# Splitting the schedule's items of a fused attention and mixing layer, and new orders for all five engines

## The reference

```
x + attention(xn) + channel_mix(xn)

attention: q, k, v = silu(conv4(xn W))           causal depthwise convolutions of 4 taps
           beta = sigmoid(xn Wb); q, k of unit length
           delta rule over chunks of tokens: attn = inverse of (I + lower part of beta k k^T),
             u = attn v - (attn k) S, o = q S + (q k^T masked) u, S = S + k^T u
           ms = (conv3, conv15, conv31 of v, per channel) @ kernel_mix, then @ channel_mixer
           weights = softmax(gelu([xn, mean|ms|, mean|o|, mean|v|] W1 + b1) W2 + b2)   per head, 3 each
           out = rmsnorm(w0 ms + w1 o + w2 v) @ Wo
channel_mix: r = sigmoid(mix_r(xn) Wr), k = relu(mix_k(xn) Wk)^2, out = r * (k Wv)
             mix(x)_t = mu x_t + (1 - mu) x_(t-1)
```

## Time and profile before

| | us |
|---|---|
| three runs, median (lowest to highest) | 3507.43 (3506.42 to 3511.52) |
| the profiled execution, span from first to last instruction | 3507.7 |
| TensorE matmul busy, share | 3329.3, 95% |
| TensorE weight load busy | 2457.7, 70% |
| VectorE busy | 3165.0, 90% |
| ScalarE busy | 2760.5, 79% |
| GpSimd busy | 826.6, 24% |
| mean granted TensorE clock | 0.984 of full |

### The profile page before, as it was taken

How to read it: one execution, slowest core, us unless ns; L and a number is a source line. 1 busy time by engine, 2 the same in 40 slices (tenths; PEclk the granted TensorE clock), 3 DMA queues, 4 the chain that set the end, 5 groups by cost and what they waited for, 6 DMA issues and landing times.

```text
span 3507.7 us, 70018 instructions
## 1 busy us (share of the span) xinstructions
PE 3329.3 (95%) x22880; PEld 2457.7 (70%) x22880; DVE 3165.0 (90%) x7841; ACT 2760.5 (79%) x9146; POOL 826.6 (24%) x1501
## 2 busy tenths in 40 slices
PE   7999999999999999999999999999999999999988
PEld 6666777677776677776677766777766777766764
DVE  6998999999988999899999989999899999999994
ACT  5777888777887778887788877788877788777775
POOL 3322221122221222211222212222112222122211
PEclk9999999999999999999999999999999999999999
DMA  6012211122211222111222112222112221112211
GB/s 187 19 39 51 51 40 34 29 51 51 50 32 29 42 51 51 38 35 29 51 51 49 32 26 46 51 51 41 33 29 51 51 50 33 33 38 51 45 30 21
DMA packets 188307, 154.92 MB, mean 44 GB/s; under 512 B 111804, under 2 KB 146108, under 8 KB 187688
## 3 DMA queue, kind: packets, MB, share of 16 engines
q0 software_dynamic: 31744, 79.70, 13.2%
q1 hardware_dynamic: 156200, 70.76, 7.7%
HBM read 51.34 MB, written 52.95 MB: 30 GB/s over the span
## 4 chain that ended last, share of the span: by engine, by line
PE 35%; ACT 22%; DVE 21%; issue 9%; DMA 8%; POOL 4%; SPq 0%; ACTq 0%; DVEq 0%; POOLq 0%
DVE my L1804 16%; PE dense L798 7%; PE dense L732 5%; PE dense L736 5%; DMA my<-prod 5%; PE dense L720 3%; ACT my L1272 3%; PE small L748 2%; ACT dense L1302 2%; PE cell L702 2%; DMA rows_out<-Bm 2%; PE cell L703 2%; PE cell L695 2%; POOL Xu L464 1%; DMA Bu<-rows_out 1%
## 5 line engine op out<-in xcount | busy, mean ns | idle before, releaser
L1804 DVE SCALAR_TENSOR_TENSOR my<-vT,mw,my 128x256 f32<-128x256 f32 x5408 | 2256.4, 482 | 38.3 <-DMA my<-prod 19.9
L422 POOL TENSOR_SCALAR vare<-xsq 128x2 f32<-128x2 f32 x32 | 6.0, 188 | 2026.7 <-ACT xsh L1022 2026.7
L798 PE MATMUL dense<-xsh,w 128*128 128x256 f32 x2016 | 474.5, 381 | 3.8
L798 PEld LDWEIGHTS dense<-xsh,w 128*128 128x128 f32 x2016 | 362.6, 190 | 70.9 <-ACT xr L1334 10.9
L1245 ACT ACTIVATE ka<-dense 128x512 f32<-128x512 f32 x64 | 38.2, 597 | 309.0 <-PE dense L720 309.0
L720 PE MATMUL dense<-xk,wfk 128*128 128x256 f32 x1024 | 245.3, 394 | 16.7 <-DVE xb L1864 14.3
L720 PEld LDWEIGHTS dense<-xk,wfk 128*128 128x128 f32 x1024 | 195.9, 196 | 67.2 <-issue 40.5
L574 PE MATMUL front<-xsh,wq 128*128 128x256 f32 x1024 | 237.6, 385 | 0.6 <-ACT raw L1060 0.6
L732 PE MATMUL dense<-wr,xr 128*128 128x512 f32 x512 | 235.3, 603 | 0.0
L574 PE MATMUL front<-xsh,wv 128*128 128x256 f32 x1024 | 229.9, 382 | 2.7 <-ACT xsh L1037 2.7
L736 PE MATMUL dense<-wfv,ka 128*128 128x512 f32 x512 | 230.2, 592 | 0.0
(11 more groups left out here) (188 smaller groups left out, 6855.9 us busy)
## 6 DMA issues: line engine op xcount, KB each, us to landing
my<-prod POOLq DMA_DIRECT2D x160, 384.0 KB, 4.2
xa<-in_x SPq DMA_DIRECT2D x32, 512.0 KB, 4.4
rows_out<-Bm SPq DMA_DIRECT2D x64, 256.0 KB, 4.2
out<-xb POOLq DMA_DIRECT2D x32, 512.0 KB, 14.8
Yq<-units_out SPq DMA_DIRECT2D x128, 32.0 KB, 2.3
w<-in_w SPq DMA_DIRECT2D x1, 2048.0 KB, 16.7
Bu<-rows_out SPq DMA_DIRECT2D x32, 64.0 KB, 3.0
units_out<-Xu SPq DMA_DIRECT2D x32, 64.0 KB, 2.5
```

Of the source, the lines that this page charges most:

```text
L798: e.matmul(by_batch(o), w1[:, k, hs(2 * pair + c)], xsh[s % 2][:, k, :, 1:1 + P], start=(k == 0), stop=False)
L1804: i = e.scalar_tensor_tensor(o, vT[s % 2][:, c, :, off:off + P], mw[:, col:col + 1], o, ALU.mult, ALU.add)
```

## The change

1. TensorE's wide products become halves, each an item of its own: `project(s, pair, c)`, `ffn_key(s, pair, c)`, `hidden(s, pair, c)` by output block; `channel_mix(s, b, part)`, `attend(s, b, part)` by two of the four contraction blocks. `ffn_out` becomes `gate_out(s, b, part)` and `value_out(s, b, part)`. The waits stand in the first half, the signal in the second. `channel_mix`'s first half needs only heads 0 and 1 of `mix_done`; `ffn_key` only the four xk entries of `mixed_in`.
2. VectorE: `short_conv(s, pair, t)` for one tap; `mix_in(s, j, c)` for one block, with xk (j=1) first; `norms_two` and the softmax in single operations.
3. ScalarE: `mix_half(s, j)` for one of xr, xk; the sums after copies are apart (`sum_tokens`, `sum_o`, `sum_ms`), and `copy_bq` is apart from `tanh_beta`.
4. New orders in the loop of TensorE, ScalarE, VectorE and GpSimd. The lists of the start and of the last step keep their order, with the new names.

```diff
-            def ffn_out(s, b):
 ...
-                for k in range(CB):
+            def gate_out(s, b, part):
+                if part == 0:
+                    e.wait_ge(*mixed_in.upto(s))
+                    if b == 0:
+                        e.wait_ge(*key_relu.upto(s, 0))
+                    else:
+                        e.wait_ge(*gated.upto(s, 0))
+                for k in range(2 * part, 2 * part + 2):
                     i = e.matmul(dense[0][:, :], xr[:, k, hs(b)], wr[:, k, :], start=(k == 0), stop=(k == CB - 1))
+                if part == 1:
+                    i.then_inc(gate_mm.sem, 1)
+
+            def value_out(s, b, part):
+                if part == 0:
+                    e.wait_ge(*key_done.upto(s))
+                    if b == 1:
+                        e.wait_ge(*gated.upto(s, 0))
+                for k in range(2 * part, 2 * part + 2):
                     i = e.matmul(dense[1][:, :], ka[:, k, hs(b)], wfv[:, k, :], start=(k == 0), stop=(k == CB - 1))
+                if part == 1:
+                    i.then_inc(value_mm.sem, 1)
...
-            def mix_in(s):
-                e.wait_ge(*mixed_half.upto(s))
+            def mix_in(s, j, c):
+                e.wait_ge(*mixed_half.upto(s, 1 - j))
```

More of the change, by code:

```diff
@@ L526, in pool_program @@
                 add_taps(i - 1, 3, 3)
+                norms_q(i - 1)
                 add_out(i - 2)
+                norms_k(i - 1)
             add_taps(NS - 1, 2, 0)
@@ L710, in state @@
                 i.then_inc(kTu_mm.sem, 1)
[L712 to L722, removed]
@@ L867, in tensor_program @@
             join_W(0)
-            project(1, 4)
+            project(1, 4, 0)
+            project(1, 4, 1)
             join_Z(0)
-            ffn_out(0, 0)
+            gate_out(0, 0, 0)
+            gate_out(0, 0, 1)
+            value_out(0, 0, 0)
+            value_out(0, 0, 1)
             half_W(0)
@@ L1424, in scalar_program @@
             copy_beta(0)
+            copy_bq(0)
             tanh_beta(0)
@@ L1505, in scalar_program @@
                 copy_beta(i - 1)
+                copy_bq(i - 1)
                 exp_logits(i - 2)
                 tanh_beta(i - 1)
-                normalize(i, 0)
                 first_taps(i - 1, 2)
@@ new lines, in vector_program @@
+                short_conv(i - 1, 2, 1)
+                short_conv(i - 1, 2, 2)
+                feature_rest(i - 2)
+                short_conv(i - 1, 2, 3)
+                feature_low(i - 2)
+                short_conv(i - 1, 3, 2)
+                short_conv(i - 1, 3, 3)
+                short_conv(i - 1, 4, 3)
+                short_conv(i - 1, 5, 1)
+                short_conv(i - 1, 5, 2)
+                short_conv(i - 1, 5, 3)
+                taps(i - 1, 1, 1, 2)
+                add_state(i - 2, 0)
@@ L2141, in vector_program @@
-                taps(i - 1, 3, 0, 2)
-                taps(i - 1, 3, 3, 5)
-                taps(i - 1, 2, 52, 53)
-                taps(i - 1, 3, 6, 8)
+                mix_in(i - 1, 1, 0)
+                mix_in(i - 1, 1, 1)
+                mix_in(i - 1, 1, 2)
+                mix_in(i - 1, 1, 3)
+                taps(i - 1, 2, 49, 51)
+                taps(i - 1, 2, 36, 37)
+                add_attention(i - 2, 1)
+                taps(i - 1, 2, 51, 53)
+                mix_in(i - 1, 0, 0)
@@ L2145, in vector_program @@
+                mix_in(i - 1, 0, 1)
+                mix_in(i - 1, 0, 2)
+                taps(i - 1, 2, 31, 32)
+                mix_in(i - 1, 0, 3)
+                taps(i - 1, 3, 1, 2)
+                taps(i - 1, 3, 0, 1)
+                taps(i - 1, 3, 4, 5)
+                taps(i - 1, 3, 3, 4)
+                taps(i - 1, 3, 7, 8)
+                taps(i - 1, 3, 6, 7)
+                taps(i - 1, 3, 10, 11)
+                taps(i - 1, 3, 2, 3)
                 turn_Y(i - 1, 0)
                 mask_W(i - 1)
-                taps(i - 1, 3, 2, 3)
```

791 lines of the change are left out of this document (469 added, 322 removed).

## The result

Slower: 3593.51 us median (3588.03 to 3599.19) against 3509.47 (3506.42 to 3515.26), ratio 1.0242 with a 95% interval of 1.0224 to 1.0261. I had forecast 3525 and a range up to 3585: it was slower, as forecast (I had given that 0.48), but the loss was 84 us where I had 18.

A forecast was written before the change was run, and what follows sets the result against it. Bound: TensorE plus short two-sided waits, VectorE 4 us behind. Quiet pass 105.4 - 1.7 + 0.8 + 2.6, less 0.2 overlap, is 106.9; with 0.9 clock 107.8 against 107.2, times 30: +18, 3525 us; range 3415 to 3585.

The forecast's parts named there:

- TensorE's gaps: TensorE's waits at half_X and key_state filled by half items, ffn_key's wait cut by 0.3: -1.7 us a pass.
- The chain of copied taps: Head 3's ScalarE products and GpSimd DMA adds end later, delaying the mask inverse_Z needs: wait 3.3 for 0.66, +2.6 us.
- GpSimd's queue: GpSimd's units end 2.5 us later, with inverse_W at 85: 0 to +2 us, taken 0.
- `turn_o` at 0.7: Both turn_o together on TensorE without the projection between; ScalarE normalises both in a row; summed wait left at 0.7 us.
- Small new waits: Waits at turn_logits, gram, the xk mix and feature_low: +0.8 us a pass, bounds -0.5 to +2.
- The sum of the quiet pass: Length of a loop pass without the clock term: 106.9 us, from 105.4 before.
- Clock: Half-rate stretches on TensorE: of 1.8 us above the quiet pass, 0.9 goes and 0.9 stays; bounds 0 to 1.7.
- my own sign of being right: Evidence expected if the forecast held; for the clock, half-rate stretches once a pass near the inverse.
- VectorE's dependent steps: Consecutive taps on the same part of my, 12 before, 37 after: +3.1 us a pass of VectorE, taken at 0.
- The semaphore that costs nothing: Skill's claim that chaining VectorE operations by semaphores costs nothing extra, making the tap term zero; the prediction disputed it.

The follow-up runs named there:

- fill_before_Z: Changed kernel with the eight products of project(i, 4, 0) done twice, once ahead of inverse_Z in its wait; 3554.37 us.
- turns_as_filler: Changed kernel with the four transposes of turn_tokens 3 done five times over, directly ahead of inverse_Z; 3556.87 us.
- interleaved_but_head2: taps_interleaved, but the 21 taps of head 2 between make_aT 1 and add_two 0 stand as in the changed kernel; 3622.94 us.
- taps_interleaved: Changed kernel with only VectorE's taps permuted between fixed neighbours, 9 dependent steps a pass where it has 37; 3659.64 us.

## Why the prediction was right or wrong

- *TensorE's gaps, -1.7*: right. The waits of 0.68 and 0.67 are gone, `ffn_key`'s 0.56 is 0.13.
- *The chain of copied taps*: right in its times, mis-sized in its price. r=1 starts 4.5 us later than before (forecast 4.1); the next two products start 6.0 and 5.9 apart (6.1), `turn_Y` starts 3.4 us later, at t 88.4 (forecast 88.7). `inverse_Z`'s wait went from 0.7 to 1.9 us, not to 3.3, because TensorE was late itself: it reached the slot 1.2 us behind my count.
- *GpSimd's queue, "taken 0"*: wrong, +0.72. The units end 2.0 us later, behind the add of r=2 (forecast 2.5), and that was not free: `inverse_W` waits for them.
- *`turn_o` at 0.7*: wrong, 0.65 + 0.51 = 1.2. Two transposes in a row wait for two normalisations in a row.
- *Small new waits, +0.8*: 0.6 (`turn_logits`) + 0.3 (`hidden`) + 0.15 (`gram`) = 1.1. For `hidden` I had no term.
- *The sum of the quiet pass*, 106.9: 106.7 in the window, 107.0 by the fit. Idle time a pass rose by 1.5 (5.6 - 4.0); the errors nearly cancel: -1.4 for the chain, +0.7, +0.5 and +0.3 for the others. That the quiet pass came out right is luck in that measure.
- *Clock, "take 0.9 us back and leave 0.9"*: the step that failed. I let the stretches behind the 64x64 products go (they did) and said that the gap at `inverse_Z` makes the others frequent; then I priced that at half of a short stretch a pass, though my own sign of being right was a stretch in each pass. 21 of the 23 in the 27 passes begin within 2 us of `inverse_Z`, five of those near it are three times as long as the one in the earlier trace rows, and the clock costs 2.4 us a pass, beyond even my bound of 1.7. Forecast -0.9, measured +1.4 (by the fits 1.0 to 2.4): 2.3 x 31 = 71 us. Of the 2.3, 1.5 is the price (2.4 for 0.9). The other 0.8 is the starting point: I took all of 1.8 us between the shortest pass and the mean for clock, of which by the fit 1.0 was. Against it stand 12 us from the quiet pass (forecast +1.5, measured +1.1); together they are 59 of the 66 us between 3525 and the measured change. That the 1.9 us of idle time before `inverse_Z` are the cause is what fill_before_Z and turns_as_filler show.
- *VectorE's dependent steps, +3.1 and hidden*: the size is right (the steps between taps take 3.2 us a pass more than before; permuting 28 of them away saves 76 us of taps and 1.0 us a pass of gaps between them, 3.5 us a pass, 0.125 each), and that VectorE doesn't set the pass is borne out: it idles 9.0 us a pass in the changed kernel (8.4 before), and the 18 undisturbed passes of interleaved_but_head2 are not shorter with 2.7 us less of it. What I did not see is that they did good: they are the breaks in which GpSimd gets in.
- *The semaphore that costs nothing*: by the Trainium skill (VectorE: DVE Perf Modes, The DRAIN you can't avoid), as I read it in the prediction, the permutation would save nothing. It saved 3.5 us a pass of VectorE's time.

## What to carry to other kernels

In this kernel a wait of 1.9 us among small products on TensorE cost about its own length again through the clock, and useless matmuls in it paid. Before you price such a wait, look how often the clock falls near the ones that are there, and price one stretch for each. Cover was moved here and not made: before moving work into a gap, look which wait it covers where it stands, and cut it finer rather than take it away. When VectorE has been made to issue back to back without a dependent step, look for GpSimd operations that have become long.

## What the runs showed of the hardware

A GpSimd operation directly behind the issue of an add was held for 4 to 7 us (3.8 to 6.9, 39 operations of taps_interleaved and interleaved_but_head2) while VectorE ran independent `scalar_tensor_tensor` with both tensors in SBUF 0.40 us apart, and ended 0.1 us behind the first break (a dependent step, 0.52) or within or just behind a run of 128x512 `tensor_tensor`. The Trainium skill (SBUF — State Buffer, SBUF: two separate sides) says that VectorE and GpSimd share one pair of ports as an exclusive lock, taken by a VectorE operation with two SBUF inputs against a GpSimd operation that reads SBUF, the loser blocking fully. The held operations agree with that, except that they were held over some ten VectorE operations in a row. What doesn't agree is that the next GpSimd operations, which read SBUF too, ran in 0.3 to 0.5 us beside the same taps: none of them was held in either run. Why only the first behind a DMA issue is held was not tried, and stays open; so does what sets the length of a half-rate stretch (3.4, 6.8, 10.2 and in one run 13.7 us).
